# The first layer norm of a fused attention and feed-forward kernel is applied by the scalar engine, as rows times deviation plus a shift, in place of two vector operations

## The chip, the cores and the metric

The kernel runs on one core of one Trainium2 chip. The metric is the device time of one execution in microseconds (us); smaller is better. Engines are called as the profile calls them: PE is the matmul engine, DVE the vector engine, ACT the scalar engine, POOL the GpSimd engine and SP the engine that here only issues transfers (DMAs).

## The reference, cut to what matters

There are 16 sequences of 256 tokens, each token a row of 256 numbers. The part that the change touches is the first line; the rest sets what waits for it.

```
def _layernorm(x, axis=-1, eps=1e-05):
    m = jnp.mean(x, axis=axis, keepdims=True)
    v = jnp.var(x, axis=axis, keepdims=True)
    return (x - m) / jnp.sqrt(v + eps)
...
x = x + xattn(_layernorm(x), ctx, ctx, Wq, Wk, Wv, Wo)   # 16 heads of 16, block-wise softmax over the context
x = x + ffn(_layernorm(x), gate_w, w1, b1, w2, b2, sw1, sb1, sw2, sb2)  # a shared expert and one of two routed ones
```

## The kernel before, in words

Every engine runs a list of instructions of its own, in the order in which its code is written, and the engines meet only at semaphores. One sequence is one iteration of about 60 us; the loop over the 16 sequences is unrolled for the first three and the last and is a hardware loop in between. The work of one iteration `i` is mixed with two other strands: the front part of sequence `i + 1` (norm, transposition, the projections to keys and queries), and the feed-forward part of earlier sequences in eight units ("up" products, relu on ACT into `h32` and `hh`, their difference `hl` on POOL, "down" products). Numbers are kept as a high and a low part, so each product is three matmuls, and most results are evacuated twice: ACT copies the high part (`high`, `mT_hi`, `xT_hi`), DVE then computes the low part (`low`, `m_lo`, `xT_lo`).

The stretch around the change is this, in the order of each engine:

- PE: 16 score products into banks of `work`, counts for the routing, the transposition of the maxima `nmax` (`maxima`), up unit 5, the transposition of `xhat` (`front_xT`, waits for `ln1_done`), the key projection, down unit 4, the query projection, and then the transposed scores (`scores_t`), which wait for `shift_spread`.
- DVE: one maximum for each score product (`maximum`), and between the 14th and the 15th the statistics of the next sequence's rows (`norm1_stats`); after the 16th `norm1_apply`, then `m_lo`, then the end of a routed unit and the routing (`finish_routed`, `route`), whose copy `ones_n` frees the bank that the key projection writes.
- ACT: relu of unit 4, `mT_hi`, relu of unit 5, the high parts of `xT`, of the keys and the queries, then 16 exponentials.
- POOL: `hl` of unit 4, `reciprocal_deviation(i + 1, 0)` (two small operations, `veps` and `rstd`), `context_low` (`c_lo`), `hl` of unit 5.
- SP: `shift(i)` waits for `m_lo`, writes `mT` to memory (`scratch_m`), waits until it has landed and reads it back in another layout into `QP`; then it sends the keys and queries of `i + 1` to memory. When the 16th transposed score product is done (`st_full`) it reads them back (`spread`: `KP` and `QP`), and the first score product of the next iteration waits for that.

`norm1_apply` before is two DVE operations of 128 rows by 256, (row - mean) * deviation, with mean and reciprocal deviation as per-row scalars from `mv` and `rstd`.

## Time and profile before

| what | value |
|---|---|
| time, median of 3 runs | 1091.39 us (1087.02, 1091.39, 1092.59) |
| time of the profiled execution | 1088.73 us |
| its span in the trace | 1086.9 us |
| busy: PE, DVE, ACT, POOL | 81%, 49%, 41%, 46% of the span |
| busy of PE's weight loads | 68% |
| mean share of full speed granted to PE | 0.924 |
| iterations | 16, of which 15 prepare a next sequence |

The span is the part of the execution that the trace covers; 1.8 us lie around it. PE at 81% is the busiest engine, but it idles at places where it waits for one particular thing, so what a shorter or longer operation is worth depends on the wait in front of which it lies. Times inside the trace count from the span's start.

### The profile page before, as it was taken

To read this page: it belongs to the slowest core of one execution; us is meant where nothing else is said; L and a number is where in the kernel's file an instruction comes from. 1 tells how busy PE (TensorE), PEld (TensorE's weight loads), DVE (VectorE), ACT (ScalarE), POOL (GpSimd) and SP (SyncE) were. 2 spreads that over 40 slices of the span, in tenths; PEclk is the share of its full clock that TensorE was granted. 3 is DMA by queue.
4 is the path that set the end of the run, shared out by engine and by line. 5 is a ranking of instruction groups with operands and counts; after the bars stand their busy time and mean duration, and the time that the engine had idled before them with its cause. 6 is when DMAs were issued, how large, how long until landed. Compare 5 with 4: busy or idle time off the path is not lost. (4 is left out here: it accounts for less than half of the span.)

```text
span 1086.9 us, 21971 instructions
## 1 busy us (share of the span) xinstructions
PE 880.9 (81%) x7654; PEld 734.8 (68%) x7654; DVE 535.5 (49%) x1089; ACT 444.3 (41%) x974; POOL 499.9 (46%) x816
## 2 busy tenths in 40 slices
PE   3377788889888898887998888889888799898564
PEld 2155566777767686776877686868677686768564
DVE  4467473464636464554736364545556373634100
ACT  3151524344444444353443444444445344344232
POOL 7242525154453536262543535363636344457333
PEclk8577887999999999999998999999999999999777
DMA  9666563819284655739192746647382909152740
GB/s 243 152 204 165 175 127 119 202 59 232 43 247 77 202 126 165 163 83 245 43 241 44 240 89 193 135 135 193 93 235 78 250 26 253 42 195 91 278 165 10
DMA packets 95745, 164.68 MB, mean 152 GB/s; under 512 B 9040, under 2 KB 81616, under 8 KB 87008
## 3 DMA queue, kind: packets, MB, share of 16 engines
q1 hardware_dynamic: 75552, 69.80, 29.4%
q10 hardware_dynamic: 9792, 71.31, 18.8%
q0 software_dynamic: 10368, 23.14, 8.4%
q8 instruction: 20, 0.33, 0.1%
q14 instruction: 13, 0.11, 0.0%
HBM read 124.30 MB, written 39.91 MB: 151 GB/s over the span
## 5 line engine op out<-in xcount | busy, mean ns | idle before, releaser
L1285 POOL TENSOR_TENSOR hl<-h,hh 128x256 fp32r<-128x256 f32 x264 | 197.3, 756 | 416.7 <-ACT hh L810 416.7
L990 DVE TENSOR_REDUCE nmax<-work 128x8 f32<-128x512 f32 x256 | 163.8, 684 | 101.5 <-PE work L468 101.5
L789 ACT ACTIVATE PT<-work 128x512 f32<-128x512 f32 x256 | 131.0, 611 | 80.4 <-PE work L483 80.4
L468 PE MATMUL work<-KP,QP 96*128 96x512 f32 x256 | 102.0, 477 | 74.6 <-DMA QP<-scratch_q 64.4
L810 ACT ACTIVATE h<-hid,bias 128x256 f32<-128x256 f32 x144 | 68.6, 476 | 191.1 <-PE hid L428 183.0
L483 PE MATMUL work<-QP,KP 128*128 128x256 f32 x512 | 104.3, 324 | 46.3 <-ACT PT L789 24.5
L996 DVE COPY T<-num 128x512 f32<-128x512 f32 x64 | 44.3, 692 | 189.0 <-PE num L501 189.0
L483 PEld LDWEIGHTS work<-QP,KP 128*128 128x128 f32 x512 | 74.5, 198 | 82.3 <-ACT PT L789 44.0
L428 PE MATMUL hid<-XS,WS 128*128 128x256 f32 x816 | 118.2, 296 | 3.1 <-DVE idle L1158 3.1
L428 PEld LDWEIGHTS hid<-XS,WS 128*128 128x128 f32 x816 | 109.6, 201 | 11.8 <-issue 6.2
L468 PEld LDWEIGHTS work<-KP,QP 96*128 96x128 f32 x256 | 46.3, 211 | 95.5 <-DMA QP<-scratch_q 43.6
L428 PE MATMUL hid<-XR,WR 128*128 128x256 f32 x768 | 110.8, 296 | 0.0
L428 PEld LDWEIGHTS hid<-XR,WR 128*128 128x128 f32 x768 | 103.8, 201 | 5.4 <-issue 2.8
L810 ACT ACTIVATE h<-hid,bias_sel 128x256 f32<-128x256 f32 x120 | 57.2, 477 | 89.3 <-PE hid L428 89.3
L618 PE MATMUL acc<-WS,hh 128*128 128x256 f32 x544 | 75.4, 282 | 0.0
L618 PEld LDWEIGHTS acc<-WR,hh 128*128 128x128 f32 x512 | 71.4, 197 | 4.7
L618 PE MATMUL acc<-WR,hh 128*128 128x256 f32 x512 | 72.4, 286 | 0.0
L501 PE MATMUL num<-PT,V 128*32 128x256 f32 x1024 | 69.2, 388 | 0.5 <-DVE T L996 0.5
L618 PEld LDWEIGHTS acc<-WS,hh 128*128 128x128 f32 x544 | 69.3, 192 | 0.1
L810 ACT ACTIVATE hh<-hid,bias 128x256 fp32r<-128x256 f32 x144 | 68.6, 476 | 0.0
L508 PE MATMUL den<-PT,bsum 128*32 128x256 f32 x1024 | 66.9, 379 | 0.0
L810 ACT ACTIVATE hh<-hid,bias_sel 128x256 fp32r<-128x256 f32 x120 | 57.2, 477 | 0.0
(197 smaller groups left out, 1544.5 us busy)
## 6 DMA issues: line engine op xcount, KB each, us to landing
WR<-wx ACTq DMA_DIRECT2D x64, 1024.0 KB, 10.0
KP<-scratch_k SPq DMA_DIRECT2D x96, 128.0 KB, 12.4
QP<-scratch_q SPq DMA_DIRECT2D x96, 128.0 KB, 13.7
scratch_k<-T SPq DMA_DIRECT2D x16, 512.0 KB, 3.9
scratch_q<-T SPq DMA_DIRECT2D x16, 512.0 KB, 2.9
wx<-WR POOLq DMA_DIRECT2D x16, 512.0 KB, 3.9
stages<-wraw POOLq DMA_DIRECT2D x24, 256.0 KB, 5.7
rowin<-queue SPq DMA_DIRECT2D x16, 260.0 KB
```

The costliest lines, as they stand in the source:

```text
L428: mm = nc.tensor.matmul(dst, R(s), R(m), start=n == 0, stop=n == len(steps) - 1)
L468: nc.tensor.matmul(bank, R(QP[0:SHIFT_ROW, p, P * t:P * t + P]), R(KP[0:SHIFT_ROW, p, :, :]), start=True, stop=True).then_inc(sem["s_full" ...
L483: mm = nc.tensor.matmul(bank[:, SEQ * t:SEQ * t + SEQ], R(KP[:, p, s, P * t:P * t + P]), R(QP[:, p, :]), start=True, stop=True)
L501: mm = nc.tensor.matmul(num[r:r + 32, j, :], V[:, t, 2 * p + s, :], PT[:, (2 * p + s) % 8, t, :], start=True, stop=True)
L508: mm = nc.tensor.matmul(den[r:r + 32, 0, :], bsum[:, p, :], PT[:, (2 * p + s) % 8, t, :], start=p == 0, stop=p == PAIRS - 1, skip_group_ch ...
L618: mm = nc.tensor.matmul(acc[:, t, :], R(h[:, k % 2, a, P * t:P * t + P]), R(w2_part(w, u, part, a)), start=first, stop=last_unit and h is ...
L789: nc.scalar.activation(PT[:, j % 8].rearrange("p t q -> p (t q)"), work[:, BANK[("st", j)], :], ACT.Exp).then_inc(sem["exp_done"], 1)
L810: last = nc.scalar.activation(dst, hid[:, k % 2, a, :], ACT.Relu, bias=b[:, a:a + 1])
L990: nc.vector.tensor_reduce(nmax[:, t, 8 * p:8 * p + 8], work[:, BANK[("s", j)], :].rearrange("q (b k) -> q b k", k=BLOCK), AX_X, ALU.max, n ...
L996: nc.vector.tensor_copy(T[:, 2 * v:2 * v + 2, :], num[:, :, :]).then_inc(sem["num_copied"], 1)
L1285: nc.gpsimd.tensor_tensor(R(hl[:, k % 2, a]), h32[:, k % 2, a], hh[:, k % 2, a], ALU.subtract).then_inc(sem["hl_done"], 1)
```

## The change

Both operations of `norm1_apply` leave DVE. POOL computes two more small things after `rstd`: `neg_mean` = -mean, and `mean_shift` = `neg_mean` * `rstd`, for the 2 numbers that each of the 128 partitions holds. ACT then computes `xhat` in two operations of 128 by 256, row * `rstd` + `mean_shift`, with both as per-row scalars. The call stands on ACT behind relu of unit 4 and ahead of the high part of the maxima; in the prologue it stands behind the first weight copy and ahead of the copy of the context.

```
+        neg_mean, mean_shift = sb("neg_mean", [P, TT]), sb("mean_shift", [P, TT])
...
+            def norm1_apply(n):
+                if type(n) is not int or n > 0:
+                    act.wait_ge(sem["xT_full"], n)
+                act.wait_ge(sem["shift1_done"], n + 1)
+                for t in range(TT):
+                    last = nc.scalar.activation(xhat[:, t, :], xin[:, t, :], ACT.Identity,
+                                                bias=mean_shift[:, t:t + 1], scale=rstd[:, 0, t:t + 1])
+                last.then_inc(sem["ln1_done"], 1)
...
                 relu(i, 4)
+                if more:
+                    norm1_apply(i + 1)
                 high(i, "mT_full", work[:, BANK[("mT", 0)], 0:P], mT[:, 0, :], "mT_hi")
...
             projection_high(0)
+            norm1_apply(0)
             context_high(0)
...
-            def norm1_apply(n):
-                if type(n) is not int or n > 0:
-                    dve.wait_ge(sem["xT_full"], n)
-                norm_apply(n, xin, xhat, 0)
...
                 maximum(i, 15)
-                if more:
-                    norm1_apply(i + 1)
                 low(i, "mT_hi", work[:, BANK[("mT", 0)], 0:P], mT[:, 0, :], mT[:, 1, :], "m_lo")
...
             norm1_stats(0)
-            norm1_apply(0)
...
                 nc.gpsimd.tensor_tensor(rstd[:, which, :], veps[:, which, :], power[:, :], ALU.pow) \
                     .then_inc(sem[f"rstd{which + 1}_done"], 1)
+                if which == 0:
+
+                    nc.gpsimd.tensor_scalar(neg_mean[:, :], mv[:, 0, :, 0], -1.0, None, ALU.mult) \
+                        .then_inc(sem["neg_done"], 1)
+                    pool.wait_ge(sem["rstd1_done"], i + 1)
+                    pool.wait_ge(sem["neg_done"], i + 1)
+                    nc.gpsimd.tensor_tensor(mean_shift[:, :], neg_mean[:, :], rstd[:, 0, :], ALU.mult) \
+                        .then_inc(sem["shift1_done"], 1)
```

On DVE, in the hardware loop, from the last maximum to the routing: before, and then of the change.

```order
L990 TENSOR_REDUCE nmax<-work 128x8 [waits s_full]
L965 REGISTER_ALU [waits xT_full]
L967 TENSOR_SCALAR xhat<-xin,mv,rstd 128x256 [waits rstd1_done]
L967 TENSOR_SCALAR xhat<-xin,mv,rstd 128x256
L947 SCALAR_TENSOR_TENSOR mT<-work,mT 128x128 [waits mT_hi]
```

```order
L998 TENSOR_REDUCE nmax<-work 128x8 [waits s_full]
L960 SCALAR_TENSOR_TENSOR mT<-work,mT 128x128 [waits mT_hi]
L1082 ISA
L1086 TENSOR_TENSOR yr<-acc,idle_sel 128x512 [waits ids_done,bias_selected,w2_done]
L1064 TENSOR_TENSOR pos_d<-apart,mask 128x2 [waits upd_done,rows_out,cnt_full]
```

The two norm operations are gone from between the last maximum and `m_lo` (the row that writes `mT`); nothing else there changes place.

On ACT, in the hardware loop, around the high part of the maxima: before, and then of the change.

```order
L810 ACTIVATE hh<-hid,bias 128x256
L748 ACTIVATE mT<-work 128x128 [waits mT_full]
L796 REGISTER_ALU
L798 REGISTER_ALU [waits hid_full]
L810 ACTIVATE h<-hid,bias 128x256 [waits w2_done,hl_done]
```

```order
L820 ACTIVATE hh<-hid,bias 128x256
L773 REGISTER_ALU [waits xT_full]
L775 ACTIVATE xhat<-xin,mean_shift,rstd 128x256 [waits shift1_done]
L775 ACTIVATE xhat<-xin,mean_shift,rstd 128x256
L749 ACTIVATE mT<-work 128x128 [waits mT_full]
```

The two norm operations now stand ahead of `mT_hi`, so `mT_hi` also waits for what they wait for.

On POOL, in the hardware loop, the change's rows from the reciprocal deviation to the low part of the context.

```order
L1282 TENSOR_TENSOR rstd<-veps,power 128x2 [waits veps1_done]
L1286 TENSOR_SCALAR neg_mean<-mv 128x2
L1290 TENSOR_TENSOR mean_shift<-neg_mean,rstd 128x2 [waits neg_done,rstd1_done]
L1273 TENSOR_TENSOR c_lo_t<-ctx_in,c_hi_t 128x512 [waits c_hi]
```

Before, `c_lo_t` stood directly behind `rstd`; two small operations have come between them.

## Rows read from the trace of the kernel before

**Rows 1.** Timeline of DVE, iteration 8: start us, length us, line, operation, [idle before].

```profile
532.07 1.26 DVE L990 TENSOR_REDUCE nmax<-work 128x8 f32<-128x512 f32 x2
533.64 1.70 DVE L967 TENSOR_SCALAR xhat<-xin,mv,rstd 128x256 f32<-128x256 f32 x2 [0.32 <-POOL rstd L1277]
535.26 0.28 DVE L947 SCALAR_TENSOR_TENSOR mT<-work,mT 128x128 fp32r<-128x128 f32 x1
```

**Rows 2.** Timeline of ACT, the same stretch.

```profile
533.75 0.28 ACT L748 ACTIVATE mT<-work 128x128 fp32r<-128x128 f32 x1 [1.88 <-PE work L474]
535.32 0.47 ACT L810 ACTIVATE h<-hid,bias 128x256 f32<-128x256 f32 x1 [1.29 <-PE hid L428]
535.69 0.47 ACT L810 ACTIVATE hh<-hid,bias 128x256 fp32r<-128x256 f32 x1
```

**Rows 3.** Timeline of POOL, the same stretch.

```profile
532.63 0.20 POOL L1274 TENSOR_TENSOR veps<-mv,eps 128x2 f32<-128x2 f32 x1
532.91 0.70 POOL L1277 TENSOR_TENSOR rstd<-veps,power 128x2 f32<-128x2 f32 x1
533.57 1.30 POOL L1268 TENSOR_TENSOR c_lo_t<-ctx_in,c_hi_t 128x512 fp32r<-128x512 f32 x1
```

**Rows 4.** Timeline of PE, from the transposition of `xhat` to the transposed scores.

```profile
535.40 0.65 PE L434 MATMUL work<-id,xhat 128*128 128x128 f32 x4 [0.26 <-DVE xhat L967]
536.40 0.39 PE L428 MATMUL work<-c_hi_t,wp_hi 128*128 128x256 f32 x1 [0.34 <-DVE ones_n L1060]
...
540.54 0.28 PE L428 MATMUL work<-a_hi_t,wp_lo 128*128 128x256 f32 x1
541.69 1.04 PE L483 MATMUL work<-QP,KP 128*128 128x256 f32 x6 [0.88 <-DMA QP<-scratch_m]
```

**Rows 5.** Timeline of SP's queue, the same iteration.

```profile
535.57 1.26 SPq L317 DMA_DIRECT2D scratch_m<-mT  x2
```

**Rows 6.** Timelines of SP's queue and of PE, between iterations 7 and 8.

```profile
492.09 2.92 SPq L301 DMA_DIRECT2D KP<-scratch_k  x6
```

```profile
514.81 0.73 PE L468 MATMUL work<-KP,QP 96*128 96x512 f32 x2 [4.36 <-DMA QP<-scratch_q]
```

**Rows 7.** Groups by line and form: count | busy us, mean ns of one | idle before.

```profile
L748 ACT ACTIVATE mT<-work 128x128 fp32r<-128x128 f32 x16 | 4.5, 278 | 37.9 <-PE work L474 37.9
L748 ACT ACTIVATE T<-work 128x512 fp32r<-128x512 f32 x30 | 18.0, 599 | 40.9 <-PE work L428 38.8 <-issue 2.1
L773 ACT ACTIVATE c_hi_t<-ctx_in 128x512 fp32r<-128x512 f32 x16 | 10.1, 634 | 52.3 <-DMA ctx_in<-ctxT 52.3
L1303 POOL TENSOR_SCALAR rows<-rows 128x2 f32<-128x2 f32 x15 | 3.8, 253 | 0.0
L967 DVE TENSOR_SCALAR rows<-x,mv,rstd 128x256 f32<-128x256 f32 x32 | 12.1, 420 | 0.6 <-POOL rstd L1277 0.6
```

**Rows 8.** Timeline of POOL: a small operation behind two waits.

```profile
482.90 0.22 POOL L1361 TENSOR_SCALAR head<-head 128x1 f32<-128x1 f32 x1 [0.16 <-POOL head L1356]
```

**Rows 9.** Timeline of DVE, the norm in iterations 1 and 14.

```profile
113.24 2.54 DVE L967 TENSOR_SCALAR xhat<-xin,mv,rstd 128x256 f32<-128x256 f32 x2 [1.24 <-POOL rstd L1277]
...
888.75 1.69 DVE L967 TENSOR_SCALAR xhat<-xin,mv,rstd 128x256 f32<-128x256 f32 x2 [0.33 <-POOL rstd L1277]
```

**Rows 10.** Timelines of DVE, ACT, POOL and PE in the prologue.

```profile
5.85 0.73 DVE L967 TENSOR_SCALAR xhat<-xin,mv,rstd 128x256 f32<-128x256 f32 x2 [1.19 <-POOL rstd L1277]
```

```profile
5.83 0.63 ACT L773 ACTIVATE c_hi_t<-ctx_in 128x512 fp32r<-128x512 f32 x1 [0.93 <-DMA ctx_in<-ctxT]
```

```profile
6.54 1.77 POOL L1268 TENSOR_TENSOR c_lo_t<-ctx_in,c_hi_t 128x512 fp32r<-128x512 f32 x1 [0.73 <-ACT c_hi_t L773]
```

```profile
8.46 0.55 PE L428 MATMUL den<-c_hi_t,wp_hi 128*128 128x256 f32 x1 [0.64 <-POOL c_lo_t L1268]
```

**Rows 11.** Stretches from first score product to `m_lo`: length, busy by engine, PE clock, DMA.

```profile
752.20:771.10 18.90, 17.92 (x132) 16.41 (x132) 16.48 (x36) 7.81 (x19) 9.44 (x12) 1.00 0.04 14
514.80:535.30 20.50, 19.46 (x132) 17.85 (x132) 16.59 (x37) 7.81 (x19) 9.43 (x12) 0.92 0.04 14
```

More of the change, by code:

```diff
@@ L133 @@
     "x2_lo r_lo finished left_step left_masked "
-    "zeroed stage_lo_pool veps1_done veps2_done rstd1_done rstd2_done c_lo hl_done x1b_done id_done "
+    "zeroed stage_lo_pool veps1_done veps2_done rstd1_done rstd2_done neg_done shift1_done c_lo hl_done x1b_done id_done "
     "upd_step upd_done sel_step sel_done bias_step bias_selected ids_done ctl_made"
```

## The prediction

> **What bounds the kernel now.** I read the timelines of the engines over one iteration of the hardware loop, each from the others' waits, because the chain that ended last covers only the end of the program. Follow iteration 8. DVE finishes the last maximum at 532.07 + 1.26 = 533.33, then waits for `rstd`, applies the norm from 533.64 to 535.34 and computes `m_lo` from 535.26 [rows 1]. ACT had the high part of the maxima ready at 533.75 + 0.28 = 534.03 [rows 2], so `m_lo` is late by 1.2 us only because the norm stands in front of it. SP starts the way of the maxima through memory at 535.57 [rows 5], behind `m_lo`'s end at 535.54. PE ends its last query product at 540.82 and the first transposed score starts at 541.69, after 0.88 us of waiting for that transfer [rows 4]. So the maxima's way is the last thing to arrive, by 0.88 us. From there the loop closes: the last transposed score releases the reading back of keys and queries on SP (492.09 in the iteration before), and the next iteration's first score starts at 514.81, after PE idled 4.36 us for it [rows 6]. Maxima, `m_lo`, transfer, transposed scores, transfer, scores: a microsecond added to `m_lo` is added to every iteration, a microsecond taken from it is gained until PE becomes the limit, which is after 0.84 (541.69 - 540.82, and a hundredth or two to start).
>
> **What the norm itself costs.** Two such operations take 2 x 0.42 = 0.84 us where POOL is quiet [rows 7], and even less as a merged pair (0.73 in the prologue [rows 10]). In the loop they take 1.70, because POOL's `c_lo` runs from 533.57 to 534.87 [rows 3], and the first of them ends only behind it. In iteration 1 another long POOL operation follows and the pair takes 2.54 [rows 9]. The last of twelve alike, with 1.69, is in [rows 9] too.
>
> **Part 1: what DVE gives up.** 1.70 us between the last maximum and `m_lo`. If nothing else held `m_lo`, it would start at 534.06, 1.20 earlier.
>
> **Part 2: what POOL does more.** `neg_mean` starts where `c_lo` starts now, 533.57 [rows 3]. It is like the small operation on 128x2 of 0.25 us [rows 7]. The product waits for two semaphores: behind such waits a small operation starts 0.16 after the one it needs [rows 8], against 0.08 between `veps` and `rstd` [rows 3]; I take 0.16. It is like `veps`, 0.20. So `mean_shift` is ready at 533.57 + 0.25 + 0.16 + 0.20 = 534.18. `c_lo` moves by 0.61, to an end near 535.48, and is hidden: the key projection starts at 536.40, when `ones_n` frees its bank [rows 4]. Without that cover it would cost 0.61. `hl` of unit 5 comes later still, behind a relu that ends after 535.69.
>
> **Part 3: what ACT does more, and who stands behind it.** DVE started 0.03 after `rstd` ended (533.61 to 533.64), so ACT starts at 534.21. No row shows an ACT operation with two per-row scalars; I build it. Copies take 0.278 for 128 columns and 0.599 for 512, both out of the matmul's memory [rows 7]: 0.385 for 256. The relu of 256 columns with one per-row scalar takes 0.47 [rows 2], so a scalar costs 0.09. The copy of the context, whose source is ordinary memory, takes 0.634 for 512 [rows 7]: 0.03 more. Two scalars: 0.385 + 0.18 + 0.03 = 0.59. Neighbours on ACT overlap by 0.10 (0.47 long, 0.37 apart [rows 2]), so each holds ACT for 0.49. Bounds: 0.37, if the second scalar is free, and 0.63 without overlap, the copy of twice the length. Behind them stands `mT_hi`: it starts at 534.21 + 0.98 = 535.19 in place of 533.75, ends at 535.47, and `m_lo` starts 0.03 later, at **535.50, against 535.26**. The wait of DVE for its own norm has been replaced by a wait for ACT's, which is 0.24 longer. Behind `mT_hi`, relu of unit 5 starts at 535.36 at the earliest, as good as now (535.32). Behind `m_lo`, `ones_n` and with it the key projection also move by 0.24, and PE's last query product to 541.06, still ahead of the transposed scores at 541.93. `xhat` is ready at about 535.29, against 535.34: nothing.
>
> **Part 4: the other iterations.** Written from the norm's start on DVE, `m_lo` now starts 1.62 after it (533.64 to 535.26), with the change 1.86. In iteration 1 it is 2.46 now (2.54 less the overlap of 0.08), since the norm was held behind two POOL operations: there the change gives 0.60 back. I count the other 14 at +0.24: +3.4.  The last iteration has no norm.
>
> **Part 5: the prologue.** ACT copies the context's high part at 5.83, POOL makes the low part until 8.31, and the first key product waits for it [rows 10]. With the change `mean_shift` is ready at 5.85 + 0.57 = 6.42, ACT is free 0.98 later, and the copy starts at 7.40, 1.57 late. POOL's `c_lo` took 1.77 here and 1.30 in the loop, so it ends between 9.41 and 9.88: +1.1 to +1.6, and nothing ahead of the keys' transfer hides it. I take +1.3.
>
> **The sum.** 3.4 - 0.6 + 1.3 = +4.1 us. Against the profiled execution's own 1088.73 us it gives 1092.8. That execution lies 2.7 below the median of the runs, 1091.39, from which it gives 1095.5. I name 1095.0, between the two and nearer to the median's.
> With the low bounds (0.22 for `neg_mean` [rows 8], 0.08 for the wait, 0.37 per ACT operation) `m_lo` starts at 535.15, -0.11; times 14, with -0.95 in iteration 1 and +0.8 in the prologue: -1.7. With the high ones (0.63 per ACT operation, 0.16 for ACT's wait as well) it starts at 535.92, +0.66: 9.2 - 0.2 + 2.0 = +11.0.
>
> **A rule that bears on it.** The norm on DVE ends only when POOL's `c_lo` has ended (1.70 in place of 0.84). The Trainium skill, SBUF — State Buffer, "SBUF: two separate sides", says that DVE in its two-port mode and POOL hold one pair of ports in turn, each for a whole instruction. The trace agrees. Its page Perfetto Trace Analysis, "Optimizing Scalar/DVE Operations", adds that an operation with a fast DVE mode is faster on DVE, and that offloading to the scalar engine may pay when DVE is saturated. By the first rule the contention is gone and the whole 1.70 us would be gained; by the second the move loses. What decides here is neither, but the place in ACT's order.
>
> **The rivals.**
> 1. *Forecast: the wait changes engines and is a little longer.* `m_lo` -0.05 to +0.33 per iteration, within 0.5%, which is 5.5 us and about what a measurement of this kernel can tell. For it: every row above. Chance 0.54.
> 2. *Slower than that: ACT's queue is the new bound.* The same place, but with an ACT operation that holds the engine for 0.55 us or more, or a slower start behind POOL. It decides from +0.34 per iteration: 14 x 0.34 + 0.7 = 5.5. At +0.45: 6.3 + 0.7 = +7.0, 1098.4. For it: no row has the operation, and the margin above my estimate is only 0.10 per iteration. Chance 0.29.
> 3. *The second scalar and the POOL steps are nearly free.* -1.7 us, 1089.7. Against it: one scalar already costs 0.09. Chance 0.07.
> 4. *The contention was the cost, and it is gone: faster.* `m_lo` would start at 534.06, and PE would be the limit after 0.84: 14 x 0.84 = 11.8 less, 1.3 back in the prologue, so 1081. It needs `mT_hi` ahead of the norm on ACT; the order has it behind. Chance 0.04.
> 5. *The clock and the transfers move it by more.* Between the first score and `m_lo` one iteration takes 18.90 us and another 20.50, with the granted clock at 1.00 and 0.92 [rows 11], the latter after PE had idled 4.36 us [rows 6]. Two such stretches more or fewer are 3.2 us. Nothing in the change lengthens that idle time, so either sign. Chance 0.06, half of it beyond 0.5%.
>
> **How the numbers follow.** The range reaches from rival 3 to the high bound: 1091.4 - 1.7 = 1089.7 and the four executions' spread of 2.8 us to either side of their middle let me open it to 1089; above, 1091.4 + 11.0 is cut to 1101, since both bounds of ACT and POOL would have to meet. Slower by over 0.5%: rival 2, part of the forecast's upper edge and half of what rival 5 has outside: 0.32. Faster by over 0.5%: rival 4 and the rest of 5: 0.06. Within: 0.62.
>
> **What would show it.** In the timeline of the changed kernel: ACT's two operations on `xhat` start about 0.57 after `c_lo`'s former place and are 0.49 apart; `mT` on ACT directly behind them; DVE idle before `m_lo` by about 2.1 us, released by ACT; the wait for `QP<-scratch_m` still about 0.88 and not zero; `c_lo` later by 0.6 with nobody waiting; the first key product near 9.8. I am wrong if `mT` is written on ACT before `xhat`, if PE's wait for the maxima disappears, or if the key projection waits for POOL's `c_lo` in the loop.

## The result, and the profile after

The changed kernel takes 1097.38 us (median of 20 runs, 1091.11 to 1109.81), the kernel before on the same chip 1097.53 (20 runs, 1080.81 to 1104.53). The ratio of the comparison is 1.0061, with a 95% interval of 1.0032 to 1.0091: slower by 0.6%, or 6.7 us (3.5 to 10). That ratio rests on the runs within 1.5% of each kernel's fastest, which are 19 of the changed kernel's 20 but, since one run of before took 1080.81, only the 9 quickest of its 20. Over all 40 runs the means are 1097.7 and 1095.9 (+1.8 us, give or take 3.3) and the medians are level. The runs scatter by 4.3 us (changed) and 6.1 us (before, standard deviations), as much as the change is worth, so the times alone do not settle whether it costs 0.6% or nothing.

The profiled execution took 1092.4 us, with a granted clock of 0.921. From its page, the span and the busy time of each engine:

```profile
span 1090.5 us, 22019 instructions
PE 887.4 (81%) x7654; PEld 740.0 (68%) x7654; DVE 513.9 (47%) x1057; ACT 458.6 (42%) x1006; POOL 505.5 (46%) x848
```

DVE has given up 2 points of the span and ACT has gained one. The rest is read at the place of the change, in iteration 8 again. Timeline of DVE, which answers to [rows 1] (there the last maximum starts at 532.07, here at 532.37, so times are compared by their distance from it):

```profile
532.37 1.25 DVE L998 TENSOR_REDUCE nmax<-work 128x8 f32<-128x512 f32 x2
535.80 0.29 DVE L960 SCALAR_TENSOR_TENSOR mT<-work,mT 128x128 fp32r<-128x128 f32 x1 [2.18 <-ACT mT L749]
536.02 0.69 DVE L1086 TENSOR_TENSOR yr<-acc,idle_sel 128x512 f32<-128x512 f32 x1
536.63 0.68 DVE L1064 TENSOR_TENSOR pos_d<-apart,mask 128x2 f32<-128x2 f32 x1
537.24 0.15 DVE L1066 SCALAR_TENSOR_TENSOR pos_b<-work,base 128x2 f32<-128x2 f32 x1
537.30 0.14 DVE L1068 COPY ones_n<-work 128x1 f32<-128x1 f32 x1
```

The norm is gone from DVE, and in its place stands a wait of 2.18 us for ACT. `m_lo` starts 3.43 behind the last maximum's start, against 3.19. Timeline of ACT, which answers to [rows 2]:

```profile
534.51 1.09 ACT L775 ACTIVATE xhat<-xin,mean_shift,rstd 128x256 f32<-128x256 f32 x2 [2.34 <-POOL mean_shift L1290]
535.51 0.26 ACT L749 ACTIVATE mT<-work 128x128 fp32r<-128x128 f32 x1
535.67 0.46 ACT L820 ACTIVATE h<-hid,bias 128x256 f32<-128x256 f32 x1
```

Timeline of POOL, which answers to [rows 3]. It ends with `hl`, which is not in [rows 3]:

```profile
533.22 0.70 POOL L1282 TENSOR_TENSOR rstd<-veps,power 128x2 f32<-128x2 f32 x1
533.90 0.23 POOL L1286 TENSOR_SCALAR neg_mean<-mv 128x2 f32<-128x2 f32 x1
534.28 0.20 POOL L1290 TENSOR_TENSOR mean_shift<-neg_mean,rstd 128x2 f32<-128x2 f32 x1
534.44 1.29 POOL L1273 TENSOR_TENSOR c_lo_t<-ctx_in,c_hi_t 128x512 fp32r<-128x512 f32 x1
536.57 1.46 POOL L1298 TENSOR_TENSOR hl<-h,hh 128x256 fp32r<-128x256 f32 x2 [0.84 <-ACT hh L820]
```

Timelines of PE and of SP's queue, which answer to [rows 4] and [rows 5]:

```profile
535.66 0.66 PE L435 MATMUL work<-id,xhat 128*128 128x128 f32 x4 [0.23 <-ACT xhat L775]
537.50 0.38 PE L429 MATMUL work<-c_hi_t,wp_hi 128*128 128x256 f32 x1 [1.18 <-DVE ones_n L1068]
...
541.73 0.28 PE L429 MATMUL work<-a_hi_t,wp_lo 128*128 128x256 f32 x1
542.27 0.73 PE L484 MATMUL work<-QP,KP 128*128 128x256 f32 x4 [0.27 <-DMA QP<-scratch_m]
```

```profile
536.12 1.26 SPq L318 DMA_DIRECT2D scratch_m<-mT  x2
```

Two things are to be seen. The wait of 0.88 for `QP<-scratch_m` has shrunk to 0.27, not because the maxima come earlier but because the query product in front of it ends later; and PE's wait for `ones_n` has grown from 0.34 to 1.18.

One row per iteration can't show a shift of tenths, so for every kernel I measured from the start of the maxima's transposition on PE, and took the median of iterations 4 to 14. The last two columns are means, from the issue of the reading back (`KP`) to the next first score, and from there to the next transposition of the maxima (without the stretch behind iteration 14, which is shorter, 16.1 us). This table is worked out from the timelines of PE, DVE and SP; it is no output of the profiler.

| us from the transposition | m_lo | ones_n | key proj. | last query ends | transp. score | reading back | KP to score | score to transp. |
|---|---|---|---|---|---|---|---|---|
| before | 1.88 | 2.82 | 3.02 | 7.44 | 8.39 | 20.02 | 21.5 | 17.8 |
| changed | 2.12 | 3.62 | 3.82 | 8.25 | 8.62 | 20.34 | 21.4 | 18.3 |
| difference | +0.24 | +0.80 | +0.80 | +0.81 | +0.23 | +0.32 | -0.1 | +0.5 |

In the prologue the three rows of ACT, POOL and PE that answer to [rows 10]:

```profile
7.70 0.61 ACT L783 ACTIVATE c_hi_t<-ctx_in 128x512 fp32r<-128x512 f32 x1
```

```profile
8.39 1.27 POOL L1273 TENSOR_TENSOR c_lo_t<-ctx_in,c_hi_t 128x512 fp32r<-128x512 f32 x1 [1.72 <-ACT c_hi_t L783]
```

```profile
9.81 0.55 PE L429 MATMUL den<-c_hi_t,wp_hi 128*128 128x256 f32 x1 [0.78 <-POOL c_lo_t L1273]
```

The first key product is 1.35 us later than before. The first score that waits for the keys is not; here it is on PE, before and then changed:

```profile
39.83 2.94 PE L468 MATMUL work<-KP,QP 96*128 96x512 f32 x5 [21.12 <-DMA QP<-scratch_q]
```

```profile
34.93 2.94 PE L469 MATMUL work<-KP,QP 96*128 96x512 f32 x5 [14.66 <-DMA QP<-scratch_q]
```

PE waits 15 to 21 us for the read-back keys and queries, and that wait covers the 1.35. In the traces below it starts at 36.2 on average in the eight kernels with the changed prologue (34.6 to 38.3), and at 38.2 in the six with the prologue of before (36.7 to 39.8).

### The profile page after: what moved, and what is told of

Same layout as the page of the kernel before. It is cut to its first block and busy times, and to the rows that moved or that the text cites. A ratio compares the mean times of both kernels' runs of the same rounds, so it can differ in the third digit from the quotient of the medians.

```text
span 1090.5 us, 22019 instructions
## 1 busy us (share of the span) xinstructions
PE 887.4 (81%) x7654; PEld 740.0 (68%) x7654; DVE 513.9 (47%) x1057; ACT 458.6 (42%) x1006; POOL 505.5 (46%) x848
## 5 line engine op out<-in xcount | busy, mean ns | idle before, releaser
L429 PEld LDWEIGHTS hid<-XS,WS 128*128 128x128 f32 x816 | 108.9, 200 | 11.2 <-issue 6.2
```

What stands on the lines that cost most here:

```text
L429: mm = nc.tensor.matmul(dst, R(s), R(m), start=n == 0, stop=n == len(steps) - 1)
```

## The experiments

**The theory.** The change lengthens one serial way: maxima, `m_lo`, memory, transposed scores, reading back, scores. It does so because `mT_hi` stands behind the norm on ACT and because two small POOL steps stand before it; each iteration pays the delay at the reading back. **The first rival.** What is slower is the key projection, 0.80 late, behind `ones_n`. **The second rival.** The serial way isn't what sets the time; PE's granted clock and the transfers between the reading back and the first score do (rival 5 of the prediction). The groups of runs were made on different chips, so only kernels of one group are compared closely. Below, "mean" is over all runs of a kernel, and the kernel before has its own mean in each group of runs made together.

### The copy that frees the bank, ahead of the slow operation

```diff
-  nc.vector.tensor_tensor(pos_d[:, :], apart[:, :], mask[:, :], ALU.mult)
   ... pos_b ...
   nc.vector.tensor_copy(ones_n[:, :], bank[:, 2:3])
+  nc.vector.tensor_tensor(pos_d[:, :], apart[:, :], mask[:, :], ALU.mult)
```

> The changed kernel, with the routing's small product pos_d moved behind the copy ones_n on the vector engine. Theory A (the collision costs a part of the loss): in the changed kernel pos_d takes 0.68 us in place of 0.15, because POOL's hl starts 0.06 us before it, and the key projection stands idle behind ones_n. With the new order ones_n should be ready about 0.55 us earlier (3.1 us from the start of the maxima's transposition on PE in place of 3.62), the key projection should start at about 3.25 in place of 3.82, and keys should be read back at about 20.25 in place of 20.34: 1 to 1.5 us less in all. Theory B (only the later m_lo counts, the key projection has slack): ones_n moves, the reading back stays at 20.34, and the time is that of the changed kernel.

Measured: 1094.43 against 1091.33 for the kernel before, ratio 1.0026 (0.9988 to 1.0064). Timelines of DVE and PE in iteration 8 of this kernel:

```profile
531.99 0.15 DVE L1066 COPY ones_n<-work 128x1 f32<-128x1 f32 x1
532.06 0.55 DVE L1067 TENSOR_TENSOR pos_d<-apart,mask 128x2 f32<-128x2 f32 x1
```

```profile
532.19 0.39 PE L429 MATMUL work<-c_hi_t,wp_hi 128*128 128x256 f32 x1 [0.59 <-DVE ones_n L1066]
```

The 0.55 is still paid, but behind `ones_n`. In the medians the key projection is 0.60 earlier (3.22), the last query product too (7.65), and the reading back only 0.07 (20.27 against 20.34). The times can't tell a difference of this size (means 1.0049 of before, and the ratio's interval holds 1). The first rival is out as the main cause: of the 0.80 nearly all lay under the wait for the maxima.

### The maxima ahead of the norm on ACT

```diff
+  high(i, "mT_full", ..., "mT_hi")
   if more:
       norm1_apply(i + 1)
-  high(i, "mT_full", ..., "mT_hi")
```

> The changed kernel, with the norm on the scalar engine put behind the high part of the maxima in the loop. Theory A (ACT's order is what costs, and the loop closes one to one): mT is written on ACT 0.4 us after the transposition's start, m_lo starts at about 0.68 in place of 2.12 (1.88 in the kernel before), xhat is ready as before since it waits for mean_shift, transposed scores start at about 7.2 in place of 8.62 (8.39 before), and with 14 iterations at -1.1 to -1.2 and the prologue at +1.35 the time is 13 to 16 us under the kernel before, ratio 0.986 to 0.988. Theory B (the transfers of keys and queries have a pace of their own): the transposed scores start earlier, the reading back lands when it did, and the ratio stays over 0.995.

Measured: 1098.71, ratio 1.0093 (1.0058 to 1.0128). `m_lo` starts at 0.68 instead of 2.12, the transposed scores at 7.15 instead of 8.62, the reading back is issued at 18.97 instead of 20.34. And the kernel is not faster. So the order on ACT is what made the maxima late, as the theory says, but taking 1.4 us out of the way gained nothing. Where it went shows between the reading back and the next transposition: 23.2 us to the score and 18.4 from there, against 21.4 and 18.3. Timelines of SP's queue and PE, and the stretch behind that first score (length, busy by engine, PE clock, DMA share, GB/s):

```profile
548.65 2.77 SPq L302 DMA_DIRECT2D KP<-scratch_k  x6
551.47 8.00 SPq L308 DMA_DIRECT2D QP<-scratch_q  x6
```

```profile
572.28 1.22 PE L469 MATMUL work<-KP,QP 96*128 96x512 f32 x2 [5.23 <-DMA QP<-scratch_q]
```

```profile
572.28:591.05 18.77, 17.90 (x119) 16.50 (x120) 14.91 (x34) 7.50 (x18) 7.92 (x11) 0.90 0.01 3
```

PE now idles 5.23 us for the keys and queries. Then it computes at a granted clock of 0.90, and the same products that take 17.0 us elsewhere take 18.77.

### The same on the kernel before: `m_lo` ahead of the norm on DVE

```diff
+  low(i, "mT_hi", ..., mT[:, 1, :], "m_lo")
   if more:
       norm1_apply(i + 1)
-  low(i, "mT_hi", ..., mT[:, 1, :], "m_lo")
```

> The kernel before, with m_lo put ahead of the norm on the vector engine; nothing is moved to another engine. Theory A (the order, not the engine, is worth the time): m_lo starts at 0.68, the norm behind it still ends only with POOL's c_lo, xhat at about 2.2 to 2.3 in place of 1.96, ones_n at about 3.1, and the transposed scores at 7.7 to 7.8 in place of 8.39 because PE's query product is now the last to end: -0.6 us in 14 iterations, 8 to 9 us under the kernel before, ratio 0.991 to 0.993. Theory B (the norm has to leave the vector engine to gain): xhat and the key projection are later by what m_lo gains, and the time is the same within 0.2%.

Measured: 1091.63 against 1091.33, ratio 1.0045 (1.0007 to 1.0083), means 1.0014. `m_lo` at 0.68, transposed scores at 7.16, reading back at 19.35, 0.67 earlier; no gain. Here the transfer did not take it: the time from reading back to score is that of before (21.5 and 21.5), so the score does come 0.67 earlier. But from the score to the next transposition it takes 18.8 us on average instead of 17.8, with nine of eleven iterations over 18.5, against five in before. PE's waits are no longer than before (3.2 us on average, 3.3), so whether the lower clock comes from the order or is chance is not told by one trace of each. With the norm on either engine an earlier `m_lo` buys nothing in this schedule.

### The maxima later still

Two maxima over a gate tile, whose results nobody reads, ahead of `m_lo` in the kernel before.

```diff
+  for n in range(2):
+      nc.vector.tensor_reduce(spare[:, n, :], gate[:, n, :]..., AX_X, ALU.max)
   low(i, "mT_hi", ..., "m_lo")
```

> The kernel before, with two reductions of 256 columns (about 0.35 us each) on the vector engine ahead of m_lo, whose results nobody uses. It prices a late m_lo. Theory A (one to one, from any cause): m_lo starts 0.7 later in all 16 iterations, the transposed scores and the reading back too, and the time is 10 to 12 us over the kernel before, ratio 1.009 to 1.011. Theory B (part of it is absorbed by the transfers): ratio under 1.005. If ones_n also meets POOL's hl, the key projection is later by 1.2 us or more, and the reading back by a little more than the transposed scores.

Measured: 1102.5, ratio 1.0133 (1.0092 to 1.0175), means +11.6 us. `m_lo` is 0.66 later (2.54), the reading back 0.81 (20.83). Timeline of DVE in iteration 8 of this kernel:

```profile
531.43 1.70 DVE L968 TENSOR_SCALAR xhat<-xin,mv,rstd 128x256 f32<-128x256 f32 x2 [0.32 <-POOL rstd L1280]
533.06 0.73 DVE L1152 TENSOR_REDUCE spare<-gate 128x4 f32<-128x256 f32 x2
533.71 0.28 DVE L948 SCALAR_TENSOR_TENSOR mT<-work,mT 128x128 fp32r<-128x128 f32 x1
```

0.81 in 15 iterations is 12.2, and 11.6 (give or take 4) came out. So later is paid about one to one, where earlier gains nothing. It is the strongest evidence that the change's +0.32 is paid too; but it was measured at 0.81, and for 0.32 it is an inference.

### The changed kernel again

> The changed kernel once more, for a second trace: what repeats is the change's, what does not is chance. Theory A (the loss is a fixed shift up to the reading back): in iterations 4 to 14, counted from the start of the maxima's transposition on PE, m_lo at 2.12, ones_n at 3.62, key projection at 3.82, transposed scores at 8.6, reading back at 20.3 to 20.4, each within 0.05 of the first trace; the wait from the reading back to the next first score and the half-clock stretches fall otherwise. Theory B (the change also lengthens the transfers or the half-clock time): the reading back to first score takes over 21.6 in the median again, and the stretch from the first score to the maxima's transposition is again longer than in the kernel before in 7 of 11 iterations.

Measured: one run of 1098.17, in a group in which the kernel before had 1089.92. All offsets of the changed kernel came again within 0.05 us (`m_lo` 2.11, `ones_n` 3.61, reading back 20.36), while the time from reading back to score was 21.8 instead of 21.4. The shift is fixed; what scatters lies behind the reading back.

### What the second scalar and the shift cost

First the scale argument alone is dropped, so the norm is rows plus shift without the deviation:

```diff
-  bias=mean_shift[:, t:t + 1], scale=rstd[:, 0, t:t + 1])
+  bias=mean_shift[:, t:t + 1])
```

> The changed kernel, but the scalar engine's operations take the shift as a per-row scalar and a scale of one as a constant: the multiplication by the deviation is left out of the first norm. It prices the second per-row scalar. My estimate of 0.09 us each says that the two operations are 0.40 to 0.41 apart in place of 0.50, and m_lo starts at 1.92 to 1.94 in place of 2.12. Rival: the price of ACT's operation comes from its source in ordinary memory; then they stay over 0.47 apart and m_lo stays over 2.06.

Then both POOL steps are left out, ACT waits for `rstd`, and the bias is the mean itself, so what is left out is the shift's computation:

```diff
-  neg_mean = -mean ; mean_shift = neg_mean * rstd   (POOL)
-  act.wait_ge(sem["shift1_done"], n + 1)
-  bias=mean_shift[:, t:t + 1]
+  act.wait_ge(sem["rstd1_done"], n + 1)
+  bias=mv[:, 0, t, 0:1]
```

> The changed kernel without POOL's two small operations: the scalar engine takes the mean itself as the shift and waits for the deviation (the shift by mean times deviation is left out of the first norm and the mean is added instead). It prices the two POOL steps. They took 0.58 from the end of the deviation to the end of the shift and 0.03 for the wait; without them m_lo should start at 1.55 in place of 2.12, which is 0.33 ahead of the kernel before (1.88). If ACT were held by something else than the shift, m_lo would stay over 1.8. The collision of pos_d with hl should also go, since pos_d then starts over half a microsecond before hl, and ones_n should be ready at 2.5 in place of 3.62.

Timelines of ACT in iteration 8, of the first and then of the second:

```profile
536.69 0.91 ACT L775 ACTIVATE xhat<-xin,mean_shift 128x256 f32<-128x256 f32 x2 [2.33 <-POOL mean_shift L1290]
537.50 0.26 ACT L749 ACTIVATE mT<-work 128x128 fp32r<-128x128 f32 x1
```

```profile
533.97 1.10 ACT L775 ACTIVATE xhat<-xin,mv,rstd 128x256 f32<-128x256 f32 x2 [1.77 <-POOL rstd L1282]
```

Without the scale the pair takes 0.91 instead of 1.09, 0.09 for each operation, and `m_lo` is 0.20 earlier (1.92). Without the POOL steps it is 0.57 earlier (1.55), which is what they hold the norm up. The reading back follows: 20.09 and 19.89 against 20.34. Their single times, 1105.54 and 1092.54, tell nothing at this size: the first kernel's way is shorter and its run is the longest of all, with a PE at half clock for 201 us of the span, against 174 in the changed kernel.

### The weights' transfer earlier, kernel before

The routed units' weights, 4 MB, are loaded by ACT's queue in the middle of the exponentials; this moves the load one visit ahead.

```diff
-WEIGHTS_VISIT = 2
+WEIGHTS_VISIT = 1
```

> The kernel before, with the four loads of the routed weights (4 MB) issued four exponentials earlier on the scalar engine. It asks what sets the landing of the keys and queries. Theory T (the 16 transfer engines are full from the weights' start on, and the keys' small packets share them until the weights have landed): the loads start about 3.3 us earlier (13.3 from the maxima's transposition in place of 16.6), the wait from the reading back to the next first score shrinks from 21.5 to 18.5 to 19.5, and with it PE's idle time and half-clock time; the time falls by 25 to 40 us, ratio 0.965 to 0.98. Theory U (the reading back has its own length, whatever the weights do): it stays at 21 to 21.6, and the ratio within 0.5% of one.

Measured: 1078.7 against 1089.92, ratio 0.9869 (0.9812 to 0.9925). The transfers of a run by name and size, with the median time from issue to landing as the last column; first of before, then of this kernel:

```profile
WR<-wx ACTq DMA_DIRECT2D x64, 1024.0 KB, 10.0
KP<-scratch_k SPq DMA_DIRECT2D x96, 128.0 KB, 12.4
```

```profile
WR<-wx ACTq DMA_DIRECT2D x64, 1024.0 KB, 9.9
KP<-scratch_k SPq DMA_DIRECT2D x96, 128.0 KB, 11.2
```

The keys land 1.2 us sooner though nothing about them has changed. Up to the reading back the offsets are those of before (19.93 against 20.02), and from there to the score it takes 20.9 instead of 21.5. That was half of what was expected, 18.5 to 19.5 and 25 to 40 us less. So the weights' load lengthens the keys' transfer, and when it goes is worth more than the whole change under study. This shows that what the second rival names limits the kernel; it doesn't show that the change acts through it.

### PE kept busy while it waits

The kernel with the maxima first, and 30 matmuls, whose result nobody reads, on PE ahead of the first score.

```diff
   front_v(i + 1)
+  for _ in range(30):
+      nc.tensor.matmul(num[:, 0, :], R(wp_hi[:, 0, 0, 0:P]), R(wp_hi[:, 0, 1, :]), start=True, stop=True)
```

> The second experiment's kernel (norm behind the maxima on the scalar engine) with 30 matmuls on PE behind the values' projection, whose results nobody uses (about 3.4 us), so that PE is not idle while it waits for the queries. Theory C (what ate the gain is partly PE's half clock: after a long idle time the granted clock falls to 0.5 and the scores and maxima behind it take 18.6 to 19.3 us in place of 17.0): in most iterations the stretch from the first score to the maxima's transposition is 17.0, the half-clock time of the whole run falls from 205 us by 30 us or more, and the time falls by 10 to 18 us against that kernel, to a ratio of 0.995 to 1.000 against the kernel before. Theory D (the clock is a symptom and only the transfers count): the stretch is shorter but the time stays within 0.3% of that kernel's 1.009.

Measured: 1086.1 against 1097.65 for before in that group (means 1086.5 and 1095.3, 0.992 give or take 0.004; the ratio formed as in the result, 1.0087, rests on 2 of the 17 runs of before, so I go by the means). The same kernel without the matmuls had 1098.71, beside a before of 1091.33: this one is 12.6 us faster, on another chip, with 3.8 us more work per iteration. Timeline of PE, and the stretch behind the score:

```profile
499.03 3.76 PE L681 MATMUL num<-wp_hi 128*128 128x256 f32 x30
503.31 0.73 PE L469 MATMUL work<-KP,QP 96*128 96x512 f32 x2 [0.52 <-DMA QP<-scratch_q]
```

```profile
503.31:520.34 17.03, 16.16 (x119) 14.86 (x119) 14.88 (x34) 7.53 (x18) 7.94 (x11) 1.00 0.07 25
```

PE waits 0.52 instead of about 5, the granted clock stays at 1.00, and ten of the eleven iterations take 17.0 us to the transposition, where eight of eleven took over 18.4. PE stood at half clock for 131 us of the span instead of 205. The idle time costs twice, once as itself and once in the clock. Whether it is the clock that takes the earlier maxima's gain is told by the last group below: with the norm on ACT it isn't.

### Earlier maxima with earlier weights

First the kernel before with both; then the changed kernel with both, and with `ones_n` and the prologue mended too.

```diff
   (kernel before)
+  low(i, "mT_hi", ..., "m_lo")         ahead of norm1_apply(i + 1)
+WEIGHTS_VISIT = 1
   (changed kernel)
+  high(i, "mT_full", ..., "mT_hi")     ahead of norm1_apply(i + 1)
+WEIGHTS_VISIT = 1
+  context_high(0)                      ahead of norm1_apply(0)
+  copy to ones_n                       ahead of the product pos_d
```

> The kernel before with m_lo ahead of the norm on the vector engine (third experiment, 1.0045 alone) and with the routed weights' loads issued earlier (0.987 alone). Theory A (the two gains are separate: the shorter way of the maxima is worth 0.67 us an iteration once the transfers do not eat it): ratio 0.978 to 0.983. Theory T (transfers set the next first score in any case, and a shorter way only makes PE idle longer): ratio 0.987 to 0.992, with more half-clock time than the kernel with early weights has (174 us).

> The changed kernel with everything that the traces point to: norm behind the maxima's high part on the scalar engine, in the prologue behind the context's copy, ones_n ahead of pos_d, and the routed weights loaded earlier. m_lo at 0.68, ones_n at about 1.6, transposed scores at 7.1, reading back at 18.9. Theory A: the reading back 1.1 us earlier counts, ratio 0.973 to 0.98. Theory T: it is given back as in the second experiment, ratio 0.987 to 0.997.

Measured: 1059.62 and 1049.45, against 1097.65 for before (means 0.9675 and 0.9577 of it; ratios formed as in the result 0.9825, 0.9739 to 0.991, and 0.9738, 0.9674 to 0.9801, again with 2 runs of before). These beat both kernels. The keys land 10.6 and 9.4 us after their issue, and in the last kernel PE waits at most 2.1 us for the first score in iterations 4 to 14. Its PE row for the transposed scores, ACT's row for the exponentials behind the weights' load, and the stretches from transposition to reading back of two iterations:

```profile
514.29 0.74 PE L484 MATMUL work<-QP,KP 128*128 128x256 f32 x4 [0.42 <-DMA QP<-scratch_m]
```

```profile
521.87 2.06 ACT L799 ACTIVATE PT<-work 128x512 f32<-128x512 f32 x4 [2.93 <-issue]
```

```profile
507.09:526.62 19.53, 16.62 (x153) 12.58 (x157) 4.99 (x11) 11.91 (x25) 14.93 (x30) 1.00 0.58 193
563.72:584.99 21.27, 18.11 (x153) 13.19 (x157) 4.99 (x11) 11.96 (x25) 15.17 (x30) 0.92 0.61 205
```

With the weights early, the maxima's place is worth 19 us on DVE (1059.6 against 1078.7). But the gain does not come by the way that was expected. In the last kernel the reading back was to be issued at 18.9. It is issued at 20.9 in the median, later than in the changed kernel. ACT idles 3.0 us at the weights' load before it goes on with the exponentials (2.3 in the changed kernel with the weights early), and PE waits 1.7 to 2.0 us for them. In four of eleven iterations the granted clock stays at 1.00 and the reading back is issued at 19.5 to 19.7, as in the first stretch above. In the other seven the clock falls behind that wait, and it is 20.9 to 21.3, as in the second. On DVE it is 0.1 earlier by the means (19.8 against 19.9). What is shorter is the time from there to the score: 19.0 and 20.0 us, against 21.0 and 20.9 with the weights early and the maxima late. The norm on ACT is in the fastest of all, but in this order only. How much of 1049 against 1060 the norm's engine has, and how much the two other edits, isn't told apart.

### The prologue's order

In the changed kernel the copy of the context goes ahead of the norm on ACT, in the prologue alone.

```diff
+  context_high(0)
   norm1_apply(0)
-  context_high(0)
```

> The changed kernel with the norm behind the context's copy in the prologue alone. In the changed kernel the copy starts at 7.70 and the first key product at 9.81, against 5.83 and 8.46 before. Expected: the copy starts at 5.8 again, the context's low part waits on POOL only for its own two small steps and ends near 8.0, and the first key product is then held by the transposition of xhat, at 9.0. If the order in the prologue were not the cause of the 1.35 us, the first key product would stay over 9.6. The loop's offsets stay those of the changed kernel.

Timeline of PE in the prologue of this kernel:

```profile
8.69 0.56 PE L429 MATMUL den<-c_hi_t,wp_hi 128*128 128x256 f32 x1
```

The first key product is back at 8.69, from 9.81; before had 8.46. The 1.1 us are the order's, and the loop is untouched (reading back at 20.36). The one run, 1105.29, with PE at half clock for 202 us, can't show a microsecond. And since the first score doesn't come earlier for it (37.95, against 34.93 in the changed kernel), the order's 1.1 us are not seen to reach the end.

### Both kernels with a steadier clock

To measure the change with less scatter, 20 such matmuls in front of the first score in both kernels; and the changed kernel with the weights early.

```diff
   front_v(i + 1)
+  for _ in range(20):
+      nc.tensor.matmul(num[:, 0, :], ..., start=True, stop=True)   (first and second)
+WEIGHTS_VISIT = 1                                                (third)
```

> The kernel before with 20 matmuls on PE behind the values' projection whose results nobody uses (about 2.3 us, in a stretch in which PE idles 2 to 4.4 us). Theory C (long idle time brings PE's clock down): from first score to the maxima's transposition 17.0 in at least 9 of 11 iterations in place of 6, half-clock time 167 down to 140 or less, time 5 to 10 us under the kernel before. Theory D (the clock does not answer to this): time within 0.3% of the kernel before or above it. Together with the next kernel it is a pair without most of the half-clock scatter.

> The changed kernel with the same 20 matmuls. Theory A (the change's cost is the fixed shift up to the reading back, 0.34 us in 14 iterations, less 0.6 in iteration 1, and 1.35 in the prologue): 5 to 6 us over the previous kernel, with m_lo at 2.12 and the reading back at 20.35. Theory B (the change costs mainly by the clock, since its PE idles more): less than 2 us over the previous kernel. Theory E (it costs over 9 us, by longer transfers): the wait from reading back to first score is longer by 0.3 us or more in the median.

> The changed kernel with the routed weights loaded earlier, as in the eighth experiment with the kernel before (median 1078.7 against 1089.9). If the change's cost is a fixed shift of 5 to 6 us, this lands at 0.5% over that kernel, median near 1084; if the earlier weights take away what made the change slow (transfers or clock), at the same 1079. The last but one experiment's 1049 must then come from the norm behind the maxima, which was worthless or worse with the late weights: this kernel should be 25 us or more above it.

Measured, with 1093.46 for before: 1081.73 (0.9907, 0.9873 to 0.9942), 1084.3 (0.9949, 0.9909 to 0.9989), and 1076.6 (0.9861, 0.9787 to 0.9934). The matmuls alone make the kernel before 1% faster. PE's time at half clock falls less than expected, from 167 us of the span to 153 (140 were expected), and to 140 in the changed kernel, from 174. They help every order alike: the changed kernel with them takes 1084.3, the one with the maxima first took 1086.1 (with 30 matmuls, on another chip), and both have 17.0 us from the score to the transposition in ten iterations of eleven. So with the clock held up the earlier maxima on ACT still gain nothing: an iteration takes 59.0 us in the trace of the one and 58.9 in that of the other. Their reading back is issued at 19.03 instead of 20.32, and the score follows 22.7 us later instead of 21.6: the transfer gives back nearly all of it.

Between the two kernels of the pair the change costs 3.1 us by the means, give or take 3.6 (12 runs each), with the reading back 0.26 later (20.06 and 20.32). 5 to 6 us were expected if the change's cost is the fixed shift, and under 2 if it is the clock; this decides for neither, and doesn't show that the change costs anything. In the traces the next first score is 0.4 later in the median but 0.1 in the mean, and iterations 4 to 14 take 59.1 and 59.0 us on average. With the weights early the changed kernel stands at 1076.6 and the kernel before at 1078.7, with scatters of 6 to 7 us and in two groups, so no cost of the change can be seen there either.

The same kernel with the maxima ahead of the norm, and the two small edits, takes 1049.45: 27 us less. Its iterations are 2.2 us shorter. The reading back is 0.2 later by the mean (20.6 for 20.3), the time from there to the score 2.0 shorter (19.0 for 21.0), and the stretch behind the score 0.5 shorter. The weights' load stands among the exponentials behind the transposed scores, so with the earlier maxima it goes 0.8 earlier, and it has landed 4.4 earlier (28.5 us from the transposition, for 32.9). Over the traces the two go together. Means of iterations 4 to 14, worked out from the issues and landings:

| kernel | weights landed, us behind the reading back's issue | KP to score |
|---|---|---|
| maxima first, weights early, on ACT, both mends | 7.9 | 19.0 |
| maxima first, weights early, on DVE | 8.8 | 20.0 |
| before, weights early | 11.2 | 20.9 |
| changed, weights early | 12.6 | 21.0 |
| changed | 14.3 | 21.4 |
| before | 15.1 | 21.5 |
| maxima first on ACT, 30 matmuls | 15.8 | 22.7 |
| maxima first on ACT | 16.5 | 23.2 |

The nine others lie in between (12.5 to 14.9, with 21.3 to 21.9). The weights' landing is itself held up by the keys' transfer, so the table alone doesn't say which causes which; the kernel before with early weights, where only their issue was moved, does. The place of the maxima pays once the weights are out of the keys' way, and it pays by moving them further out, not by an earlier reading back.

## Why the prediction was off, step by step

- **What bounds the kernel now.** Half right. Later is paid about one to one (the kernel with later maxima, 0.81 later). That a microsecond taken away "is gained until PE becomes the limit" failed: 1.05 and 0.67 at the reading back gained nothing. With the norm on ACT the keys' transfer took longer by 1.7 us; with it on DVE the transfer took as long as before, and the stretch behind the score 1.0 longer at a lower clock. Rival 4, the contention gone and 11.8 us won, would not have come even with the other order: that kernel took 1098.7.
- **Part 1.** Right: 1.70 us gone from DVE, and a longer wait in its place.
- **Part 2.** Right to hundredths: `neg_mean` 0.23 for 0.25, the product 0.20, `mean_shift` ready 0.56 behind `rstd`'s end (534.48 less 533.92) against 0.57 forecast (534.18 less 533.61); `c_lo` 0.6 later, and nobody waits for it.
- **Part 3, ACT.** Right: 0.59 and 0.50 apart for 0.59 and 0.49, `m_lo` +0.24 as named, in every iteration of the hardware loop. The mechanisms of rivals 2 and 3 fell on these rows; that the time came out where rival 2 had it, over 0.5%, is not by its mechanism, which needed +0.34 per iteration at `m_lo`. The Trainium skill, ScalarE: Activation LUTs, section "What ACT_TABLE_LOAD costs", gives an ACTIVATE 186 ns plus 0.833 ns for each column and about 93 ns for each per-row operand, an estimate of 0.585 us here. The trace agrees, with 0.59, and with 0.09 less without the scale.
- **Part 3, who stands behind it: the step that failed.** "Behind `m_lo`, `ones_n` and with it the key projection also move by 0.24" was wrong: they moved by 0.80. The half microsecond comes from `pos_d`, a product of two columns with two inputs, which takes 0.68 here. Before, it ran at 536.06 in 0.15, just ahead of POOL's `hl`, as these timelines of the kernel before show, of DVE and of POOL:

```profile
536.06 0.15 DVE L1056 TENSOR_TENSOR pos_d<-apart,mask 128x2 f32<-128x2 f32 x1
...
536.31 0.67 DVE L1062 TENSOR_TENSOR pos<-pos_b,pos_d 128x2 uint32<-128x2 f32 x1
```

```profile
536.23 1.48 POOL L1285 TENSOR_TENSOR hl<-h,hh 128x256 fp32r<-128x256 f32 x2 [1.36 <-ACT hh L810]
```

  Before, the operation caught behind `hl` was `pos`, which stands behind `ones_n`. With the change `hl` starts at 536.57 and `pos_d` at 536.63, so it is caught, and `ones_n` with it. I had placed every operation by its start, and had not asked what each would then meet on POOL. The copy ahead of `pos_d` takes it back. The Trainium skill, SBUF — State Buffer, "SBUF: two separate sides", which the prediction had used for the norm, says that a DVE operation with two inputs in SBUF, too, is blocked for the whole of a POOL operation that reads SBUF and started first. The trace agrees: `pos_d` has two such inputs and took 0.68 for 0.15.
- **What the miss cost.** Little, but it used up the cover. The last query product ends 0.81 later, the wait for the maxima falls to 0.27, and the low part of the keys and queries (`T`), later as well, stops the transposed scores once more, as this row of the changed kernel's PE shows:

```profile
543.42 1.69 PE L484 MATMUL work<-QP,KP 128*128 128x256 f32 x8 [0.41 <-DVE T L960]
```

  The reading back is 0.32 later, not 0.24; with the copy ahead of `pos_d` it is 0.25 later. So the collision explains nearly all of the 0.08 by which the term was too small.
- **Part 4.** Iteration 1 gave 0.61 back at `m_lo`, forecast 0.60. "The other 14 at +0.24" holds for the hardware loop; in iterations 0 and 2 `m_lo` came 0.46 and 0.44 later. In iteration 1 PE's granted clock was 0.67 behind `m_lo` (0.76 before), and the transposed scores started 0.57 later all the same, so it isn't shown that the 0.60 reached the end.
- **Part 5.** Right for the first key product, at 9.81, +1.35 for +1.3. Wrong in counting it: the first score, which waits for the keys and queries, came no later (34.93, against 39.83 before, and earlier on average over all the traces), so the term +1.3 is not seen to be paid.
- **The sum.** The forecast was +4.1 us and within 0.5%; the comparison gave +6.7 (3.5 to 10), 0.6%. The term "the other 14 at +0.24: +3.4" was too small: with the 0.32 measured it is 4.5, and the sum as it was built is 4.5 - 0.6 + 1.35 = 5.2 us, or 0.48%. That is still within 0.5%, so this step alone does not carry the time over the line. And the terms of iteration 1 and the prologue are not seen at the end; without them 4.5 are left, about what was named, which is luck as far as those two cancel. The 2.2 us up to 6.7 are not explained and are within the scatter; over all runs the difference, +1.8 (-1.5 to 5.0), holds 4.5 as well as nothing. The profiled execution moved by 3.7 us, 1088.73 to 1092.4, and not by the fixed shift alone: its first transposition of the maxima is 2.0 us earlier, while iterations 4 to 14 are 0.7 longer each, 0.2 of it at the score and 0.5 in the stretch behind it, at a lower clock; whether the change has a part in that is open. That 1095.0 was named and 1097.4 measured says less: the kernel before itself had 1091.39 in its first three runs and 1097.53 in the twenty beside the changed one.
- **Rival 5.** Its mechanism was taken for too small. I gave it 3.2 us. But weights one visit earlier are worth 14 us, and 20 idle matmuls 11 us, with the change nowhere in them. "Nothing in the change lengthens that idle time" held (2.9 us on average in iterations 4 to 14 of the changed kernel, 3.3 in before), so the scatter it makes has no sign, but it is larger than the change.

## What to carry to other kernels

When work moves to another engine, look at its place in that engine's queue before its duration: here the norm's engine moved `m_lo` by 0.24 us, and its place ahead of or behind the maxima by 1.4. After shifting a start by a few tenths, walk down both engines that share a port once more, for a tiny operation may now be caught behind a long one. And a shorter serial way is not yet a gain: if what it waits for is a transfer that a larger one slows, the time can turn into idle time of PE, and that may lower the clock on top. Nor is a delay in a prologue a loss before it is followed to the first thing that waits longest.

## What was not expected of the hardware

- A DVE product of 128x2 with two inputs took 0.68 us instead of 0.15, when POOL had started a 0.75 us operation 0.06 ahead of it.
- PE's clock fell after its longest waits. In the kernel before, the four iterations in which PE had idled for 4.10 to 4.36 us ahead of the first score needed 18.6 to 19.3 us for the following stretch, and the three with 1.95 to 2.07 us needed 17.0. In between, 3.62 us brought 18.6, but 3.28 and 3.49 us 17.0. In the changed kernel two iterations with nearly the same wait went both ways, as these stretches show, the first after 3.21 us of idling and the second after 3.27:

```profile
633.34:650.36 17.02, 16.15 (x120) 14.85 (x120) 14.87 (x34) 7.53 (x18) 7.95 (x11) 1.00 0.07 24
692.19:710.77 18.58, 17.71 (x119) 16.31 (x120) 14.91 (x34) 7.52 (x18) 7.91 (x11) 0.91 0.02 6
```

  All of them have the same 120 products (one is missing in the record of the second); 1.00 is the 2.4 GHz level throughout, and 0.91 a mean over a part at 1.2 GHz. With the weights early, waits of 2.52 and 2.55 us went both ways too. What decides between such neighbours isn't settled by these runs.
- Useless matmuls made two kernels faster: by 12.6 us (30 of them in each iteration, maxima first, the two on different chips) and by 11 us (20 of them, kernel before).
- A 4 MB load issued 3.6 us earlier brought another queue's keys 1.2 us sooner and the kernel 1.3%.
